# Second expert's weight copies behind the last projection, the router's exponential later in the last sequence, and another order of loads and norms at the end

## The reference

```python
scores = jax.nn.softmax(jnp.einsum('bsd,ed->bse', x, router_w), axis=-1)
gate_vals, sel_idx = jax.lax.top_k(jnp.swapaxes(scores, 1, 2), capacity)   # capacity = 129
tokens = x[b_idx, sel_idx]
h = jnp.einsum('becd,edh->bech', tokens, w1) + b1[None, :, None, :]
h = jax.nn.gelu(h, approximate=False)
y = jnp.einsum('bech,ehd->becd', h, w2) + b2[None, :, None, :]
out = jnp.zeros_like(x).at[b_idx, sel_idx].add(y * gate_vals[..., None])
x = _layernorm(x + _L0_ffn_ref(x, ...), axis=-1)
```

## Time and profile before

| | us |
|---|---|
| median of 3 runs | 891.51 (891.24 to 892.38) |
| the profiled execution's own time | 894.26 |
| its span, first to last instruction | 892.5 |
| PE busy | 821.0 (92%) |
| DVE busy | 606.6 (68%) |
| ACT busy | 532.7 (60%) |
| POOL busy | 468.0 (52%) |

### The profile page before, as it was taken

The page is one execution under the profiler, slowest core; times in us unless marked ns, Lnnn a source line. Parts: engine busy times, 40 slices in busy tenths (PEclk is TensorE's granted clock), DMA queues, the critical chain, the costliest instruction groups (busy, mean ns, idle before and its releaser), DMA issues.

```text
span 892.5 us, 17252 instructions
## 1 busy us (share of the span) xinstructions
PE 821.0 (92%) x5908; PEld 615.5 (69%) x5908; DVE 606.6 (68%) x2067; ACT 532.7 (60%) x1048; POOL 468.0 (52%) x640
## 2 busy tenths in 40 slices
PE   4779999999999999998778999999999999999994
PEld 3534454454645454433258999999999999999993
DVE  5668777788788778899858854546464554646466
ACT  2247767667586766666647445555565656555546
POOL 6458565666655565344658356445444444545343
PEclk9779999999999999999899999999999999999998
DMA  4863434536352424610253223335243342613275
GB/s 144 221 191 112 133 107 151 155 107 185 123 149 95 159 91 156 192 64 11 89 199 109 30 44 60 91 83 145 40 103 69 53 129 40 150 28 52 31 208 188
DMA packets 89574, 100.12 MB, mean 112 GB/s; under 512 B 8592, under 2 KB 82960, under 8 KB 89360
## 3 DMA queue, kind: packets, MB, share of 16 engines
q1 hardware_dynamic: 72128, 77.66, 27.8%
q0 software_dynamic: 12368, 16.52, 11.4%
q10 hardware_dynamic: 4992, 4.85, 1.8%
HBM read 65.38 MB, written 33.23 MB: 110 GB/s over the span
## 4 chain that ended last, share of the span: by engine, by line
PE 72%; DVE 14%; ACT 6%; issue 3%; POOL 1%; DMA 1%; SPq 1%; ACTq 1%; DVEq 0%; POOLq 0%
PE y_ps L1434 22%; PE h_ps L1416 18%; PE av_ps L816 7%; PE st_ps L784 5%; DVE n_ps L648 5%; PE n_ps L799 5%; PE stage_ps L835 3%; PE stage_ps L877 3%; PE stage_ps L843 3%; PE tp_ps L1389 2%; ACT pt L539 1%; DVE nmax L648 1%; DVE best_at L182 1%; DVE row_pool L184 1%; DVE nm L680 1%
## 5 line engine op out<-in xcount | busy, mean ns | idle before, releaser
L648 DVE CUSTOM_DVE_ANT_0 n_ps<-n_ps,tri 128x512 f32<-128x512 f32 (+3 forms) x512 | 238.6, 519 | 72.5 <-PE n_ps L799 70.5
L539 ACT ACTIVATE pt<-st_ps 128x512 f32<-128x512 f32 x320 | 184.4, 602 | 60.5 <-PE st_ps L784 45.5
L1434 PE MATMUL y_ps<-w_parts,h_hi 128*128 128x256 f32 (+1 forms) x1152 | 215.8, 281 | 2.0 <-POOL h_lo L1187 1.6
L1226 ACT ACTIVATE g<-h_ps,b 128x384 f32<-128x384 f32 (+1 forms) x192 | 104.1, 542 | 164.8 <-PE h_ps L1416 138.4
L1434 PEld LDWEIGHTS y_ps<-w_parts,h_hi 128*128 128x128 f32 (+1 forms) x1152 | 172.6, 177 | 5.9 <-issue 1.9
L1416 PE MATMUL h_ps<-tt_hi,w_parts 128*128 128x384 f32 (+1 forms) x768 | 169.7, 323 | 3.7 <-issue 2.0
L1198 POOL DMA_INDIRECT acc<-y,tok_no x61 | 98.1, 1608 | 140.7 <-DVE y L1342 132.7
L1326 DVE TENSOR_TENSOR h_lo<-g,h_hi 128x384 fp32r<-128x384 f32 (+1 forms) x176 | 90.1, 513 | 115.4 <-ACT h_hi L1231 95.6
L468 POOL TENSOR_SCALAR_AFFINE_SELECT pt<-pt 128x256 f32<-128x256 f32 (+1 forms) x320 | 109.8, 361 | 105.4 <-ACT pt L539 104.6
L1434 PE MATMUL y_ps<-w_parts,h_lo 128*128 128x256 f32 (+1 forms) x576 | 161.5, 280 | 0.0
L784 PE MATMUL st_ps<-w_parts 99*128 99x512 bf16 (+3 forms) x512 | 125.7, 307 | 17.5 <-ACT pt L539 15.9
(11 more groups left out here) (209 smaller groups left out, 1091.0 us busy)
## 6 DMA issues: line engine op xcount, KB each, us to landing
w_parts<-part_d SPq DMA_DIRECT2D x186, 128.0 KB, 2.8
w_raw<-in_w SPq DMA_DIRECT2D x16, 1024.0 KB
part_d<-w_raw SPq DMA_DIRECT2D x96, 128.0 KB, 2.2
w_raw<-in_xt SPq DMA_DIRECT2D x8, 512.0 KB, 4.2
res<-in_x SPq DMA_DIRECT2D x8, 512.0 KB, 4.7
x<-res SPq DMA_DIRECT2D x8, 512.0 KB, 3.3
acc<-res SPq DMA_DIRECT2D x8, 512.0 KB, 5.1
fin<-acc SPq DMA_DIRECT2D x4, 512.0 KB, 4.5
```

The source lines that it names most:

```text
L539: nc.scalar.activation(pt[:, slot % PT_RING, n % UP, :], st_ps[at % ST_RING][:, :], ACT.Exp, scale=S_SCALE).then_inc(exp_done, 1)
L648: ins = nc.vector.tensor_tensor_reduce(out=src[:, h, :], in0=src[:, h, :], in1=mask, scale=-1.0, scalar=-BIG_NEG, op0=ALU.add, op1=ALU.min ...
L1226: nc.scalar.activation(g[:, at % G_RING, 0:cols], h_ps[at % H_RING][:, 0:cols], ACT.Gelu, bias=b1[:, e, n:n + 1]).then_inc(g_done, 1)
L1434: ins = nc.tensor.matmul(y_ps[at % Y_RING][0:rows, 0:C], x[:, q % 2, m, toks], w[e % 2][:, m, :], start=i == 0, stop=i == len(terms) - 1)
```

## The change

Three tables of numbers move work within the queues; nothing is computed in another way.

1. The two copies of expert 1's weights on ACT go from places 1 and 12 of iteration 8 to places 24 and 25, behind "ot", "proj" and "rstd" of sequence 7, and the four low pieces on DVE from place 11 to 26.
2. In iteration 7 alone "lexp" (of sequence 6) goes from place 29 to 38 and "score" from place 32 to 39, behind the last round of the picking.
3. In the end part the loads of sequences 3, 4, 5 go behind those of 0, 1, 2; norms 6, 7, 0, 1, 2 and 3 come earlier against the "down" and "spread" steps; the three "spot" steps are spread over slots 2, 4, 6 of job 22, and POOL's iota becomes a stage of its own, one job earlier.

```diff
-NEXT_CUT_AT, NEXT_LOW_AT = ((B, 1), (B, 12)), (B, 11)
+NEXT_CUT_AT, NEXT_LOW_AT = ((B, 24), (B, 25)), (B, 26)
+SCORE_AT = {'lexp': (3, 8), 'score': (3, 9)}
...
                 for gg, kk, stage, ahead, n in STAGES:
+                    if i == B - 1:
+                        gg, kk = SCORE_AT.get(stage, (gg, kk))
...
-FINISH = [((NQ - 2, 0), "load", 6), ((NQ - 2, 1), "load", 7)] + [((NQ - 2, 2), "load", b) for b in ON_CHIP]
-FINISH += [((NQ - 2, 4), "norm", 6), ((NQ - 2, 7), "norm", 7)]
-FINISH += [((NQ - 2, 8), "load", b) for b in (0, 1, 2)]
-FINISH += [((NQ - 1, 0), "norm", 0), ((NQ - 1, 4), "norm", 1)]
-ON_CHIP_AT = [((NQ - 2, 0), "spot", b) for b in ON_CHIP]
...
+FINISH = [((NQ - 2, 0), "load", 6), ((NQ - 2, 1), "load", 7), ((NQ - 2, 2), "norm", 6), ((NQ - 2, 4), "norm", 7)]
+FINISH += [((NQ - 2, 8), "load", b) for b in (0, 1, 2) + ON_CHIP]
+FINISH += [((NQ - 2, 8), "norm", 0), ((NQ - 2, 9), "norm", 1), ((NQ - 1, 4), "norm", 2)]
+ON_CHIP_AT = [((NQ - 3, 1), "place", 0)] + [((NQ - 2, 2 + 2 * n), "spot", b) for n, b in enumerate(ON_CHIP)]
+ON_CHIP_AT += [((NQ - 1, 7), "spread", ON_CHIP[0]), ((NQ - 1, 7), "norm", ON_CHIP[0])]
```

More of the change, by code:

```diff
@@ L935 @@
 ON_CHIP = CHUNKS[JOBS[NQ - 1][1]]
-FINISH = [((NQ - 2, 0), "load", 6), ((NQ - 2, 1), "load", 7)] + [((NQ - 2, 2), "load", b) for b in ON_CHIP]
-FINISH += [((NQ - 2, 4), "norm", 6), ((NQ - 2, 7), "norm", 7)]
-FINISH += [((NQ - 2, 8), "load", b) for b in (0, 1, 2)]
-FINISH += [((NQ - 1, 0), "norm", 0), ((NQ - 1, 4), "norm", 1)]
-ON_CHIP_AT = [((NQ - 2, 0), "spot", b) for b in ON_CHIP]
-ON_CHIP_AT += [((NQ - 1, 7), "spread", ON_CHIP[0]), ((NQ - 1, 8), "spread", ON_CHIP[1]), ((NQ - 1, 8), "spread", ON_CHIP[2])]
-ON_CHIP_AT += [((NQ - 1, 8), "norm", b) for b in (2,) + ON_CHIP]
+FINISH = [((NQ - 2, 0), "load", 6), ((NQ - 2, 1), "load", 7), ((NQ - 2, 2), "norm", 6), ((NQ - 2, 4), "norm", 7)]
[3 more added lines that the diff above has]
+ON_CHIP_AT += [((NQ - 1, 7), "spread", ON_CHIP[0]), ((NQ - 1, 7), "norm", ON_CHIP[0])]
+ON_CHIP_AT += [((NQ - 1, 8), stage, b) for b in ON_CHIP[1:] for stage in ("spread", "norm")]
 NORMS = [b for _, stage, b in FINISH + ON_CHIP_AT if stage == "norm"]
@@ L1188, in _ @@
                                         h_hi[:, q % 2, n, 0:cols].bitcast(F32), ALU.subtract).then_inc(g_lo, 1)
-            elif stage == "spot" and q == ON_CHIP[0]:
+            elif stage == "place":
                 nc.gpsimd.iota(place[:, :].bitcast(I32), pattern=[[1, T]], base=0, channel_multiplier=0).then_inc(placed, 1)
@@ L1346, in _ @@
                 dve.wait_ge(tp_done, KC * NQ)
-                if n == 0:
+                if q == ON_CHIP[0]:
                     dve.wait_ge(placed, 1)
```

## The result

| | us |
|---|---|
| before, median of 10 | 891.56 (nine of them 891.17 to 892.38, the tenth 1307.58) |
| changed, median of 10 | 896.14 (893.77 to 902.43) |
| ratio | 1.0056, 95% interval 1.0037 to 1.0075 |
| profiled execution of the changed kernel | 893.77, span 892.0 |
| forecast | 890.8, range 888.5 to 893.6 |

The changed kernel is slower by 5.0 us (4.6 by the two medians), and above the range. Its times also lie far apart, over 8.7 us where nine of the ten of before lie within 1.2; before's tenth, at 1307.58, is left out of the ratio. The profiled execution is the fastest of the ten, and the profiled one of before was 2.7 us above its median, so the two traces laid side by side show no loss.

A forecast was written before the change was run, and what follows sets the result against it. PE, never resting from about 479 to 870 us, was taken to bound the kernel. The terms -0.5 + 0 + 2.0 + 0.5 - 2.7 = -0.7 us took 891.51 to 890.8 us, range 888.5 to 893.6.

The forecast's parts named there:

- What bounds the kernel: PE never rests from about 479 to 870 us; shifting that stretch's start shifts everything behind it one for one.
- The shares: Last sequence of attention: sequence 6's shares leave DVE's unbroken rounds for a wait of 1.14 us; -0.5 us.
- The weight copies on ACT: Passage to job 0: the copies held nothing up before and are hidden behind PE's projection after; 0 us.
- The low pieces: Passage: DVE's 2.53 us now precede `tt_lo`, less 0.55 us swallowed by the logits' wait for POOL; +2.0 us.
- Rule and row: Low pieces beside POOL's inverse deviation: skill's exclusion rule made the term +3.2 us; a profile row showed DVE unheld, and was kept.
- The granted clock: PE's rests before DVE's last round and job 0 may bring half speed; +0.5 us for both (0 to +2.0).
- Rival (a): PE's clock stays low for longer, with job 0's opening at 1.2 GHz; +2.2 us, 893.7 us, chance 10%.
- The end part: End: DVE's reordered queue fills its waits, if loads land in time; -2.7 us (-3.2 to -1.0).
- Rival (d): End part gives nothing because a load comes late and DVE waits in order; +2.0 us, 893.5 us, chance 10%.
- Rival (b): Passage: sequence 7's projection keeps full clock, 1.7 us less; -2.4 us, 889.1 us, chance 15%.
- signs of being wrong: First gelu coming less than 1 us later, or DVE waiting for a load in the end part.
- two bad ends at once: Rule for the range: two terms at their bad ends together come to +1.5 us, 893.0 us.

The follow-up runs named there:

- e2_score: Kernel before with only the exponential and shares of sequence 6 moved later; 894.13 us, ratio 1.0036.
- e10_warm: As e2_score, plus 28 throw-away transposes on PE ahead of its wait for the last cast; ratio 1.0007.
- e1_cut: Kernel before with only the second expert's weight copies and low pieces moved to their late places; 894.75 us, ratio 1.0036.
- e11_job0: As e1_cut, plus 34 throw-away transposes on PE ahead of job 0's first matmul; ratio 1.0034.
- e12_free: Kernel before with the new end part, but loads 3, 4, 5 in their old place and sequence 2's load fetching sequence 3's finished rows (wrong output); ratio 0.9976.
- e3_end: Kernel before with only the end part in the new order of loads and norms; 890.39 us, ratio 0.9988.
- e5_warm: As e2_score, plus 14 throw-away transposes on PE ahead of its wait for the last cast; ratio 0.9991.
- e4_shares: Kernel before with only the shares of sequence 6 moved behind the last cast, the exponential left in its place; ratio 0.9986.
- e6_loads: As e3_end, but with the loads of sequences 3, 4, 5 between those of 0 and 1; ratio 0.9987.

## Why the prediction was wrong, point by point

**What bounds the kernel** held: the three places lie outside PE's unbroken stretch, and what they gain or lose arrives at the end one for one.

**The shares, -0.5 us.** A is 0.53 us shorter where only the shares move, but B gives it back. The mechanism (DVE alone sets this stretch) was half of the truth: PE had only 0.26 us to wait for the last cast. The step that failed, though, is the sentence that the freed 2.7 us of ACT and PE are "worth nothing by itself". Alone on the kernel before they come to a loss of some 3.6 us (1.07 + 2.5): ACT's freed time sent POOL into DVE's logits in four of the five traces with the whole of edit 2 (+1.07 us), and PE's became a rest before the thread it works on (+2.5).

**The weight copies on ACT, 0 us.** Right: in the changed kernel `av_sb` waits 4.41 and `o_t` 2.34 us for PE, and `tt_hi` 0.73.

**The low pieces, +2.0 us.** The low pieces do delay the thread, and the term came out at 2.4. The wrong step is "PE's first unit is done about 1 us before that gelu": it was done 0.07 us before the table load, which stands behind the wait for it, so the 0.55 us that the logits had waited for POOL gave nothing back. Rule and row, which I had weighed as against each other, were both read too simply. In the changed kernel the low pieces started first (457.99) and took their 2.49 us, while POOL's inverse deviation, started 0.18 us behind them, was stretched to 1.42 us from the 1.04 it took in the kernel before, beside `tt_lo`, which reads one of its inputs from PSUM:

```profile
458.17 1.42 POOL L500 TENSOR_TENSOR rstd<-ve,half 128x4 f32<-128x4 f32 x1 [3.03 <-DVE ve L710]
```

In e2_score POOL started first, and DVE's logits waited it out. The Trainium skill, "SBUF — State Buffer", adds under "Who interferes with whom" that the order of issue decides who is held; both rows agree with that sentence. I had cited the exclusion without it, and looked for it only at the step that was moved, not at those that the move lets run into each other.

**The granted clock, +0.5 us.** The mechanism was named and its size was not. For the rest before the last cast I allowed 0 to +1.0 and it cost 2.5 (e2_score against e10_warm); I had counted 1 us of PE's work behind it, and it was the transposes, the mirror and all 32 matmuls of the last sums, 5.5 us by e10_warm's B. For the rest before job 0 I allowed 1.0 hidden microsecond that isn't hidden; it cost 0.5 (e1_cut against e11_job0) and 1.0 (the changed kernel against e11_job0). Rival (a) is what happened in kind, and at a second place that it didn't name.

**The end part, -2.7 us.** The walk through DVE's queue was right in one trace: without the late load it gave 2.5 us (e12_free). The step that failed is "needed at 871.9" against "lands at 870.6". In the changed kernel DVE came to it at 871.9, but the load was issued at 867.3, took 5.78 us and landed at 873.1. The margin of 1.3 us rested on 3.8 us, the best of eight loads; sequence 2's own had taken 4.93 in the kernel before, and over the sixteen traces it takes 3.7 to 5.8. Rival (d), at 10%, was the better half of the truth: -1.1 us on the median.

**Rival (b)**, the projection at full clock, is probably what the kernel before does in most of its runs of the first and third session. C is 8.9 us in ten of the traces here, and 10.55 in the profiled execution of before, whose B is also 0.7 us longer than e3_end's. Together that is 2.35 of the 2.7 us by which that execution stood above its median. I read the 5.50 us projection as the kernel's own, though the excess was known, and so booked as a chance of gain what the median most likely had already.

**What I had named as the signs of being wrong** were both there: DVE waits for a load, and the first gelu comes 0.40 us earlier instead of 2 later. The second of them says little, since rounds and projection were earlier by more than that; D is the fair measure, and it grew by 3.4.

**The range** ended at 893.6, from single terms added as if the changed order left each engine's neighbours alone. Its rule that two bad ends at once come to +1.5 us also leaves out the worst pair: +1.5 for the clock and +1.7 for the end part make +2.5, 894.0. The sum that the experiments give for the three edits, 891.6 + 5.3 = 896.9, is near the measured 896.1.

## What to carry to other kernels

An engine that is freed from a wait off the critical path isn't a neutral result: ask what it now does at that time, with whom it collides, and whether PE comes to rest just ahead of work on the thread. A gain that rests on a transfer landing in time is to be priced with what that very transfer took and how far its landings spread, not with the shortest of its line; here the margin was below the spread, and over half of the gain was lost on the median. And where the profiled execution stands apart from the median, find the stage that explains it before using that stage's durations.

## What the runs showed of the hardware

- After 3.8 us of rest PE ran the small matmuls that followed at a granted clock of 0.50, and of 0.60 over the next 7.6 us (e2_score). With the rest filled by 28 throw-away transposes (0.12 us each) it was 1.00 (e10_warm). With 1.84 us of rest left, the sums behind it took 4.50 us instead of 2.36 (e5_warm).
- In the same kernel code the low clock falls at different places from execution to execution. In two sessions of four all traces but one had the projection at 1.2 GHz for most of its length. The windows of PE are of e4_shares and of e3_end, which have the same instructions there; e6_loads, with e3_end's instructions up to the end part, is like e4_shares (C 12.28).

```profile
451.00:458.00 7.00, 6.14 (x18) 0.51 0.28 83
```

```profile
451.00:458.00 7.00, 5.54 (x30) 1.00 0.33 94
```

- That costs 3.3 us in C, and it would account for the 3.1 us by which the medians of before differ between the first and the second session, which ran on the same chip. What makes PE fall into it in one session and not in another stays open.
- The gelu's table load took 1.28 us and stands in ACT's queue behind the wait for PE's first unit. It began 0.07 us after PE's signal in the kernel before and in e3_end, and ACT stood idle 0.65 to 1.64 us ahead of it in the kernels with edit 1.
- A load of 512 KB landed 3.7 us after its issue at best and 12.3 at worst. Most of that range is loads standing behind one another: in e1_cut five, issued about half a microsecond apart, took 3.8, 4.8, 5.7, 7.2 and 8.1 us. A load's sixteen pieces mostly land together, and now and then the last comes 1 to 2.8 us after the others.
